# Another order for the start of an attention and expert kernel: norms, transposes and first slot

## The reference

```python
def attn(query, ctx):            # 16 heads of 16
    Q, K, V = (heads(t @ W.T + b) for t, W, b in ((query, Wq, bq), (ctx, Wk, bk), (ctx, Wv, bv)))
    scores = where(causal, Q @ K.T / sqrt(16), -inf)
    return (softmax(scores) @ V).reshape(B, S, 256) @ Wo.T + bo

x = x + attn(layernorm(x), ctx_1024)
x = x + ffn(layernorm(x))        # 8 experts, the best 2 of each row, and a shared one
```

## Time and profile before

| | us |
|---|---|
| median of 3 runs | 506.07 (505.5 to 507.34) |
| the profiled execution | 505.84 |
| its span in the profile | 504.1 |
| PE busy | 455.0 (90%) |
| DVE busy | 309.2 (61%) |
| ACT busy | 210.1 (42%) |
| POOL busy | 193.2 (38%) |
| mean granted clock of PE | 0.977 |

### The profile page before, as it was taken

One profiled execution on the slowest core, in us unless ns is written; L12 is line 12 of the kernel. 1 busy time (PEld: TensorE's weight loads), 2 busy tenths in 40 slices (PEclk: granted clock), 3 DMA queues, 4 the chain that ended last, 5 costly groups with the idle time before them and its releaser, 6 DMA issues.

```text
span 504.1 us, 10169 instructions
## 1 busy us (share of the span) xinstructions
PE 455.0 (90%) x3098; PEld 316.2 (63%) x3099; DVE 309.2 (61%) x651; ACT 210.1 (42%) x419; POOL 193.2 (38%) x204
## 2 busy tenths in 40 slices
PE   7668999999999999997769799999999999999993
PEld 6444444464446544473346356499999999999852
DVE  4975656647574766546865596865455455455437
ACT  1235566616665275716773452522332232332210
POOL 4130346305451145401332001226666666666420
PEclk9976999999999999999999999999999999999997
DMA  8934121231124221220098910113444434434379
GB/s 273 255 83 127 38 90 40 96 126 63 66 73 135 73 74 53 89 90 3 4 358 285 416 38 11 32 33 54 73 64 73 74 63 72 75 63 70 37 193 337
DMA packets 45574, 53.84 MB, mean 107 GB/s; under 512 B 7760, under 2 KB 41872, under 8 KB 44912
## 3 DMA queue, kind: packets, MB, share of 16 engines
q1 hardware_dynamic: 34320, 39.77, 24.1%
q0 software_dynamic: 7488, 10.31, 12.6%
q10 hardware_dynamic: 3744, 3.47, 2.4%
HBM read 27.09 MB, written 13.67 MB: 81 GB/s over the span
## 4 chain that ended last, share of the span: by engine, by line
PE 66%; ACT 11%; DVE 11%; DMA 6%; issue 5%; SPq 1%; DVEq 0%; ACTq 0%; POOLq 0%
PE set_a L618 7%; ACT attention L1063 6%; PE set_b L648 6%; PE set_a L915 5%; PE set_a L916 5%; PE set_a L914 5%; PE set_a L669 4%; PE set_a L842 4%; PE set_b L638 4%; DVE attention L1293 3%; PE set_b L933 3%; PE set_a L823 3%; PE set_b L935 3%; PE set_b L934 3%; PE set_b L852 2%
## 5 line engine op out<-in xcount | busy, mean ns | idle before, releaser
L1293 DVE TENSOR_REDUCE attention<-set_a 128x2 f32<-128x1024 f32 (+2 forms) x96 | 96.0, 1041 | 32.3 <-PE set_a L620 30.3
L1063 ACT ACTIVATE attention<-set_b 128x512 f32<-128x512 f32 (+1 forms) x176 | 88.5, 570 | 60.4 <-PE set_b L638 47.8
L525 POOL TENSOR_SCALAR_AFFINE_SELECT attention<-attention 128x512 f32<-128x512 f32 x64 | 40.9, 652 | 120.4 <-ACT attention L1063 120.4
L584 POOL DMA_INDIRECT sum_rows<-moe,token_of x39 | 61.8, 1585 | 43.8 <-issue 29.6
L638 PE MATMUL set_b<-attention 99*128 99x512 bf16 (+3 forms) x256 | 59.9, 307 | 12.2 <-ACT attention L1063 9.7
L618 PE MATMUL set_a<-attention 96*128 96x512 bf16 (+3 forms) x256 | 63.9, 315 | 5.2 <-DVE attention L1293 3.6
L576 POOL DMA_INDIRECT e_x<-normed_rows,token_of x39 | 39.4, 1011 | 62.9 <-DVE token_of L1494 36.5
L1162 ACT ACTIVATE moe<-set_a 128x384 f32<-128x384 f32 x39 | 19.2, 492 | 105.0 <-PE set_a L916 105.0
L1519 DVE TENSOR_TENSOR moe<-set_a,moe 128x384 f32<-128x384 f32 x39 | 21.8, 558 | 62.8 <-ACT moe L1162 61.2
L618 PEld LDWEIGHTS set_a<-attention 96*128 96x128 bf16 x256 | 25.7, 101 | 47.3 <-DVE attention L1293 16.8
L914 PE MATMUL set_a<-wup_hi,e_xT_hi 128*128 x156 | 53.0, 340 | 0.0
(11 more groups left out here) (166 smaller groups left out, 837.7 us busy)
## 6 DMA issues: line engine op xcount, KB each, us to landing
attention<-attention SPq DMA_DIRECT2D x182, 64.0 KB, 2.6
wup<-in_wupT SPq DMA_DIRECT2D x2, 3072.0 KB, 14.2
sum_rows<-attention SPq DMA_DIRECT2D x2, 2048.0 KB, 12.8
wup<-sum_rows SPq DMA_DIRECT2D x8, 512.0 KB, 7.0
attention<-in_ctxT SPq DMA_DIRECT2D x7, 512.0 KB, 6.0
w_down<-in_wdnT SPq DMA_DIRECT2D x3, 1024.0 KB, 5.1
x_res<-in_x SPq DMA_DIRECT2D x4, 512.0 KB, 6.9
out<-x_res ACTq DMA_DIRECT2D x8, 256.0 KB, 4.0
```

The costliest lines, as they stand in the source:

```text
L584: g.indirect_dma_start(acc[i], bass.IndirectOffsetOnAxis(token_of[:, t:t + 1], 0), e_y[:, t % 2, :], None, compute_op=ALU.add).then_inc(ad ...
L1063: nc.scalar.activation(pT[k][:, h:h + heads, :], bank(par)[:, 0:heads * (S - k * P)], ACT.Exp).then_inc(b_free, 1)
L1293: v.tensor_reduce(dst, src, AX.X, ALU.max, negate=True).then_inc(a_free, 1)
```

## The change

Five edits, all ahead of the loop over batches; the loop and what follows are left alone.

1. The first slot has its own table `FIRST`: `R` 0 to 2, then `S` and `R` in turn; the rest is as in `SLOT` without `PV`. The wait for the free bank moves from the head of the slot to `S` 0.
2. All four norms run on DVE ahead of the first reduction. The transposes of batch 2 come after four `R` jobs, those of batch 3 after all six, ahead of the first `maxima`. All use the same two banks, so each waits for the copy of the one before.
3. ACT's copies follow that order, with one `Exp` of a single column of `ident` after the copy of batch 1, and `part2(1)` after the first row of maxima.
4. POOL's first `remainders(1)` waits for the first `max_parts`. SP issues the loads of contexts 1 to 3, `wo` and `bo` after the 14 pieces of groups 0 and 1; PE waits for them at the end of the slot.
5. Products of constants, 48 after the projections (`keep_busy(6)`) and 8 ahead of the first `maxima` (`keep_busy(1)`), into the bank `pv_bank`.

```diff
+        FIRST = [("R", 0), ("R", 1), ("R", 2), ("S", 0), ("R", 3), ("S", 1), ("R", 4), ("S", 2), ("R", 5)]
+        FIRST += [(kind, n) for kind, n in SLOT if kind == "MAX" or kind == "S" and n > 2]
...
-        LN_JOB, LN_PAIR, MAX_0 = (0, 1, 2, 4), (0, 0, 1, 0), 3
+        LN_JOB, MAX_0 = (0, 1, 2, 3), B
...
-            for b in range(1, B):
-                load_ctx(b, ld_ctx)
-            sp.dma_start(wo, woT.rearrange("(c p) n -> p c n", p=P)).then_inc(ld_o, DMA)
-            sp.dma_start(bo_bc, bo.partition_broadcast(P)).then_inc(ld_o, DMA)
...
             for part in range(3):
                 stack_part(1, 0, 0, part)
+            for b in range(1, B):
+                load_ctx(b, ld_ctx)
+            sp.dma_start(wo, woT.rearrange("(c p) n -> p c n", p=P)).then_inc(ld_o, DMA)
+            sp.dma_start(bo_bc, bo.partition_broadcast(P)).then_inc(ld_o, DMA)
             stack(2, 1)
...
+            pool.wait_ge(mparts_ready, 1)
             remainders(1)
...
             def ln_transposes(b):
                 pe.wait_ge(xs_ready, b + 1)
+                if b:
+                    pe.wait_ge(b_free, LN_JOB[b - 1] + 1)
...
-                        last = tr(Bk[:, 2 * LN_PAIR[b] + c, j * P:(j + 1) * P],
+                        last = tr(Bk[:, c, j * P:(j + 1) * P],
...
             project_v(2, 2, 0, cT)
-            pe.wait_ge(consts, 4)
+            keep_busy(6)
             ln_transposes(1)
             pe.wait_ge(rows_in[0], DMA * 12)
             for j in range(A_GRP):
                 rowmax_scores(0, j, 3 + j, 3 + j)
-                if j == 1:
+                if j == 3:
                     ln_transposes(2)
-            pe.wait_ge(b_free, LN_JOB[2] + 1)
+            ln_transposes(3)
+            keep_busy(1)
             maxima(MAX_0, B + 2, 1, first=True)
-            ln_transposes(3)
             pe.wait_ge(fills, 3)
-            pe.wait_ge(ld_ctx, DMA * (B - 1))
-            pe.wait_ge(ld_o, DMA * 2)
...
                     elif kind == "S":
+                        if j == 0 and order is FIRST:
+                            pe.wait_ge(b_free, B_GRP0)
...
-            pe.wait_ge(b_free, B_GRP0)
-            slot(0, 0, B_GRP0, B_GRP0, (3 + A_GRP, 3 + A_GRP), wait_rows=(rows_in[1], DMA * 12), pv=False)
+            slot(0, 0, B_GRP0, B_GRP0, (3 + A_GRP, 3 + A_GRP), wait_rows=(rows_in[1], DMA * 12), order=FIRST)
+            pe.wait_ge(ld_ctx, DMA * (B - 1))
+            pe.wait_ge(ld_o, DMA * 2)
             pe.wait_ge(a_free, A_PRO)
...
             ln_copy(1)
+            nc.scalar.activation(credit[:, 2:3], ident[:, 0:1], ACT.Exp)
+            ln_copy(2)
             part1(1, 1, ((0, 1), 1))
-            ln_copy(2)
+            ln_copy(3)
+            max_rows(MAX_0, B + 2, 0)
             part2(1)
-            max_rows(MAX_0, B + 2, 0)
-            ln_copy(3)
...
             normalised(2, lambda j: xs[0][:, j:j + 1, :]).then_inc(xs_ready, 1)
+            dve.wait_ge(b_full, LN_JOB[1] + 1)
+            normalised(3, lambda j: xs[1][:, j:j + 1, :]).then_inc(xs_ready, 1)
...
                 max_parts(3 + (g + 1) * A_GRP, g + 1)
-                if g == 0:
-                    dve.wait_ge(b_full, LN_JOB[1] + 1)
-                    normalised(3, lambda j: xs[1][:, j:j + 1, :]).then_inc(xs_ready, 1)
```

More of the change, by code:

```diff
@@ L121, in build @@
         std = sb("std", [P, T])
-        credit = sb("credit", [P, 2])
+        credit = sb("credit", [P, 3])
         KB = 256
@@ L319, in build @@
         MAX_AT = 9
-        assert [n for kind, n in SLOT if kind == "R"] == list(range(A_GRP))
-        assert [n for kind, n in SLOT if kind == "S"] == list(range(S_N))
+        FIRST = [("R", 0), ("R", 1), ("R", 2), ("S", 0), ("R", 3), ("S", 1), ("R", 4), ("S", 2), ("R", 5)]
+        FIRST += [(kind, n) for kind, n in SLOT if kind == "MAX" or kind == "S" and n > 2]
+        for order in (SLOT, FIRST):
+            assert [n for kind, n in order if kind == "R"] == list(range(A_GRP))
+            assert [n for kind, n in order if kind == "S"] == list(range(S_N))
         A_TILES = [range(i, min(i + 3, C * QT)) for i in range(0, C * QT, 3)]
         NA = len(A_TILES)
-        LN_JOB, LN_PAIR, MAX_0 = (0, 1, 2, 4), (0, 0, 1, 0), 3
+        LN_JOB, MAX_0 = (0, 1, 2, 3), B
         B_GRP0 = B + 1
@@ L671, in project, with keep_busy @@
                 return last
+            def keep_busy(turns):
+                with pe.Fori(0, turns):
+                    for _ in range(8):
+                        mm(pv_bank[:, 0:P], identb[:], beforeb[:], start=True, stop=True)
             pe.wait_ge(consts, 4)
-            with pe.Fori(0, 8):
-                for _ in range(8):
-                    mm(pv_bank[:, 0:P], identb[:], beforeb[:], start=True, stop=True)
+            keep_busy(8)
             ln_transposes(0)
@@ L693, in _, with slot @@
                 rowmax_scores(0, j, 3 + j, 3 + j)
-                if j == 1:
+                if j == 3:
                     ln_transposes(2)
-            pe.wait_ge(b_free, LN_JOB[2] + 1)
+            ln_transposes(3)
+            keep_busy(1)
             maxima(MAX_0, B + 2, 1, first=True)
-            ln_transposes(3)
             pe.wait_ge(fills, 3)
-            pe.wait_ge(ld_ctx, DMA * (B - 1))
-            pe.wait_ge(ld_o, DMA * 2)
-            def slot(g, count, n_b, par_b, rows=None, projection=None, wait_rows=None,
-                     pv=True):
+            def slot(g, count, n_b, par_b, rows=None, projection=None, wait_rows=None, order=SLOT):
                 at = 0
@@ L713, in slot @@
                     pe.wait_ge(*wait_rows)
-                for kind, j in SLOT:
+                for kind, j in order:
                     if kind == "R" and rows:
                         rowmax_scores((g + 1) % NG, j, rows[0] + at + j, rows[1] + at + j)
-                    elif kind == "PV" and pv:
+                    elif kind == "PV":
                         probs_v((g - 1) % NG, count - 1, j)
                     elif kind == "S":
+                        if j == 0 and order is FIRST:
+                            pe.wait_ge(b_free, B_GRP0)
                         if j == 0:
@@ L1011, in ln_copy @@
                 act.wait_ge(b_full, LN_JOB[b] + 1)
-                copy(xnT[:, :, b * S:(b + 1) * S], pair(Bk, LN_PAIR[b])).then_inc(b_free, 1)
+                copy(xnT[:, :, b * S:(b + 1) * S], Bk[:, 0:C, :]).then_inc(b_free, 1)
             def stack_part(g, a, part):
@@ L1030, in max_rows @@
                                     ).then_inc(max_in, DMA)
+            act.wait_ge(consts, 1)
             ln_copy(0)
```

## The result

The changed kernel takes 501.03 us, the median of 4 runs (500.69 to 502.17); the kernel before, run beside it, 506.7 (505.5 to 507.39). The ratio is 0.9895 [0.9867, 0.9922]. So it is faster by about 1%, 5.3 us by the ratio, where 7.4 were forecast; 501.03 lies inside the range of 497.0 to 501.8 and 2.6 us above the forecast. The profiled execution is the slowest of the four: 502.17 us, with a span of 500.3 against 504.1.

The account below looks back on a forecast made before the run. PE is nearly full from the loop's first projection at 50.83 us, so the start, a chain through DVE and then a detour, bounds the gain. 1.3 + 4.2 + 1.9 = 7.4 us off 505.84 gives 498.4 us, range 497.0 to 501.8.

Parts of the forecast that it names:

- The head, up to the second transposes: Start of the kernel: the 48 constant products fit in a PE wait and cost nothing; gain taken as 0.
- Up to the first maxima: 1.3 us: Batch 1 transposes to first `maxima`: kept clock and held-back POOL bring `maxima` to 34.05 instead of 35.35, 1.3 us won.
- From the maxima to the slot: 4.2 us: First `maxima` to the slot's first `R`: 0.39 us instead of 4.60, the slot starting at 34.4; 4.2 us won.
- The slot: 1.9 us won: First slot, up to the loop's first projection: 10.88 us before, both chains now ending at 43.4 to 43.5; 1.9 us won.
- I take 3.0 from the issue at 35.1: In the slot: maxima's DMA issue to `S` 0, between 2.2 (a later row, 248.56 to 250.76) and 3.8; `S` 0 at 38.1.
- 0.4 of waiting for `S` 0: In the slot's DVE chain: 0.4 us of waiting for `S` 0, within a chain of 9.1 us.
- What comes next: nothing lost: Loop's start: late group 3 pieces make ACT stand 2.6 us; about 0.4 may reach ACT, nothing taken, up to 1 in range.
- So I let the clock stand.: From 26 to 38 us, PE at some 60%, a third of it transposes: the granted clock was assumed not to fall.
- rival 1: Clock falls between 26 and 38 us or stays low after the head; time 500.9, at worst 504; chance 0.15.
- rival 2: Moved loads delay the last group 1 pieces, so `S` 0 begins 2.3 us later; time 500.7; chance 0.10.
- Rival 3: In the loop, group 3 pieces land 2 to 4 us later than 50.5, holding ACT; 500.4 to 502.4; chance 0.10.
- Every later event 7 to 7.5 us earlier, to the end: Sign to look for in the changed profile: the whole loop shifted 7 to 7.5 us earlier, with no shrinking along it.

Follow-up runs that it names:

- the new order alone: Kernel before with only the new order of norms, transposes, copies and maxima, plus the one-column `Exp`; no hold, fillers or moved loads: 503.29 us, ratio 0.9951.
- loads back: Changed kernel with the five loads (contexts 1 to 3, `wo`, `bo`) ahead of the 14 pieces again: 499.78 us, and 500.14 us when repeated.
- `SLOT`'s order with loads back: Changed kernel with the five loads in their old place and the first slot in `SLOT`'s order without `PV`: 501.35 us, ratio 0.9907.
- the kernel with the most filler: Changed kernel, loads in old place, constant products: 24 and 8 after group 0's `R` 1 and 2, 16 before `maxima`, 8 after slot's `R` 1 and 2: 501.32 us.

## Why the prediction was right and wrong

- **The head, up to the second transposes: 0.** Right. The 48 products ended at 22.96 in a wait, and their lack cost 0.5 us further on in one execution, which the next step had counted.
- **Up to the first maxima: 1.3 us.** Right: 35.35 to 34.08 is 1.27. The stall of 0.4 for the transposes of batch 2 is 0.54; the small instructions took 0.90 to PE's start, with the hold shown to make it so.
- **From the maxima to the slot: 4.2 us.** Right: 4.60 before, 0.32 now. It is the bulk of the change: with the new order alone it is 0.32 as well (35.60 to 35.92).
- **The slot: 1.9 us won.** This step failed: it lost 0.5. "I take 3.0 from the issue at 35.1" was 3.25, inside its bounds of 2.2 and 3.8, so `S` 0 was only 0.27 us late against the sum (38.37 for 38.1). What the sum had wrong is the stretch behind `S` 0: 5.3 us (38.1 to 43.4) were forecast, 7.39 measured, of which about 1.5 go with the clock, low for most of 38.4 to 41.6; on DVE the "0.4 of waiting for `S` 0" became gaps of 1.46 us ahead of 39.84 and 0.75 ahead of 41.55. And the cause of the wait was missed. The row that I priced it by, lies in a stretch in which the DMA engines do nothing (share 0.01 in 246 to 251 us of the kernel before), and I did not look whether the same holds where the transfer was going. The Trainium skill, "DMA: Bandwidth & Descriptors", section "Issuing engines are not separate DMA queues", says that DMAs issued from SP and from ACT run on the same 16 engines and interleave; the runs agree, with 2.34 us and 3.25. With the loads in their old place the length comes out as forecast, 8.94 and 8.97 for 9.0 to 9.1, but in part by luck: `S` 0 came 0.7 us sooner than the sum had it (37.41), and the stretch behind it took 5.88 us at full clock, 0.6 more than the sum had.
- **What comes next: nothing lost.** Right. ACT stood 3.08 us (forecast 2.6) and its first exponential, at 53.27, was no later against the loop than before (7.51 us behind it, both times). With loads back it was 0.70 late (51.50) and PE lost nothing.
- **"So I let the clock stand."** Half wrong. It stood to 38 us, and fell after the idle 1.31 us. This was rival 1 by its result, 500.9 us, with the loads of rival 2 as the reason for the gap; only that rival 2 had them delay the last pieces of group 1. These did land at 31.1 instead of 29.4, inside my bound of 31.3, with no effect; what the loads held up was the maxima's DMA. The range took in both rivals, which is why 501.03 lies in it. The Trainium skill, "TensorE: Matmul & The Clock Gate", Part 4, has transposes not count as activity. The runs don't bear it out: in 28 to 34 us, which holds the transposes of batches 2 and 3, the clock was 0.72 in four profiles and 1.00 in the other nine, and three of the four had PE's stream of the changed kernel up to there. In one of them, `SLOT`'s order with loads back, `R` products were slow already ahead of the transposes:

```profile
29.57 0.53 PE L623 MATMUL set_a<-attention 96*128 96x384 bf16 x1
...
30.00 1.92 PE L611 MATMUL set_b<-ident,attention 128*128 128x128 f32 x8
```

What makes it fall stays open.
- **Rival 3, the pieces of group 3.** Not at work in the changed kernel. The last landed 4.9 us behind the loop's start; the runs show no loss up to 7.2 us, 0.10 at 7.53, 0.31 at 7.73 and 0.35 at 7.77.
- **Every later event 7 to 7.5 us earlier, to the end.** Wrong in size: 5.07 to 246 us, then 3.8. The loop passes a lead on untouched to 246 us. What shrinks it later is the granted clock: 0.3 us in 245 to 260, where only the kernel before kept 1.00, and 0.8 in 280 to 290, where a second execution of the changed kernel lost nothing. The medians differ by 5.7 us, the profiled spans by 3.8.

What stays open: why 2.5 to 2.8 us at the loop's start (loads back against the changed kernel) come out as 1.05 in the medians (the profiled spans differ by 3.2 and 1.8); why the clock falls in 245 to 260 us in every changed profile; and why the kernel with the most filler, at full clock through its start, is not among the fastest, beyond the one execution whose last transfer was slow. The best version is the changed kernel with the five loads in their old place, 499.78 and 500.14 us: under the kernel before clearly, and under the changed kernel by the pooled medians.

## What to carry to other kernels

A transfer that is moved to "later" meets other transfers there: list which small DMA on the critical path is issued while it is still moving, and move bulk loads to where nothing urgent is in flight, or leave them. Where a wait on PE gets longer, price the clock behind it as well as the wait; here 0.9 us of waiting cost 2.4 in the slot, some 1.5 of it by the clock. And if the clock falls by chance, compare kernels by stretches at the same clock and by many runs, since one profile may be a lucky one.

## What the runs showed of the hardware

- A 12 KB DMA on ACT's queue takes 2.33 to 2.39 us from the start of its issue to the product that waits for it in seven profiles in which no bulk load was in flight any more, and 3.15 to 3.25 in three where it was issued at 35.1 to 35.3 us, with 1.9 MB of loads keeping the DMA engines full, though these stood on another queue. Issued at 35.63, nearer to their end, it took 2.71. In two kernels with constant products just ahead of `S` 0 (3.12 and 2.76 us) PE's own work held the product back longer than the DMA did.
- A subtraction of 128x16 on DVE takes 0.18 us alone and 1.01 beside a two-input operation on POOL. The Trainium skill, "SBUF — State Buffer", section "Who interferes with whom", has a VectorE instruction with two SBUF inputs contend with a GpSimd instruction that reads SBUF, over a port that the two share; the runs agree.
- The granted clock fell in some executions and not in others of the same instructions. In 28 to 34 us it is 0.72 in four profiles and 1.00 in nine; constant products did not exclude a fall (0.75 in 38 to 42 us with 32 more of them).
